# A four-layer kernel with one hand-written order for each engine: the order behind the weight search rewritten, with the chains of batches 2 and 3 between the tiles in small pieces

## What is computed

```python
x = x + _L0_xattn_ref(_layernorm(x), ctx, Wq, bq, Wk, bk)   # attention over the features
x = x + _L0_ffn_ref(_layernorm(x), w_fc, w_proj)            # 256 -> 1024 -> 256, squared relu
x = x + _L1_xattn_ref(_layernorm(x), fside, ctx)            # gated MLP in int8, weights per batch
x = x + _L1_ffn_ref(_layernorm(x), Wq, keys, e_down, e_up)  # product-key lookup of experts

# _L0_ffn: both weights are first quantised: for each block of 64 the best of 16 scales is searched
# _L1_xattn, twice per batch (gate_up, then down):
s = jnp.sqrt(jnp.maximum(amax_x, EPS) / jnp.maximum(amax_w, EPS)); xs = x / s; ws = w * s
x_q = jnp.clip(jnp.round(xs / x_scale), -QMAX, QMAX); w_q = jnp.clip(jnp.round(ws / w_scale), -QMAX, QMAX)
h = x_q @ w_q.T * x_scale * w_scale.T
# _L1_ffn, per token and head (4 heads, 2048 experts):
s1, i1 = top_k(sim1, 8); s2, i2 = top_k(sim2, 8)
final_scores, pk_idx = top_k((s1[:, None] + s2[None, :]).reshape(64), 8)
hidden = silu(x . e_down[idx]) * relu(final_scores); out = sum(hidden * e_up[idx])
```

## Time and profile before

| | us |
|---|---|
| median of 3 runs (lowest, highest) | 453.34 (451.8, 455.67) |
| profiled execution, its own time | 452.77 |
| its span, first to last instruction | 451.0 |
| busy in the span: PE, DVE, ACT, POOL | 372.2, 334.8, 248.1, 164.0 |
| share of TensorE's full clock, mean | 0.924 |

### The profile page before, as it was taken

The page is one execution under the profiler, slowest core; times in us unless marked ns, Lnnn a source line. Parts: engine busy times, 40 slices in busy tenths (PEclk is TensorE's granted clock), DMA queues, the critical chain, the costliest instruction groups (busy, mean ns, idle before and its releaser), DMA issues.

```text
span 451.0 us, 8463 instructions
## 1 busy us (share of the span) xinstructions
PE 372.2 (83%) x3278; PEld 277.3 (61%) x3278; DVE 334.8 (74%) x870; ACT 248.1 (55%) x371; POOL 164.0 (36%) x203
## 2 busy tenths in 40 slices
PE   2987897689979997997469959979899789996467
PEld 1554664345434456996357848858688677885356
DVE  4998599957995975367866976597868799569830
ACT  4889959778868982017545454665565754020000
POOL 3355844478979996000010132060502324011000
PEclk9998999869999999998759969999899998999598
DMA  9910000000000002400000000000000000000000
GB/s 265 362 61 2 0 0 1 0 1 1 0 1 1 0 0 55 134 1 1 0 2 1 1 1 1 1 14 1 13 0 15 1 15 1 13 1 3 12 15 12
DMA packets 11144, 11.42 MB, mean 25 GB/s; under 512 B 608, under 2 KB 10592, under 8 KB 11104
## 3 DMA queue, kind: packets, MB, share of 16 engines
q1 hardware_dynamic: 11104, 10.88, 7.6%
HBM read 9.83 MB, written 1.05 MB: 24 GB/s over the span
## 4 chain that ended last, share of the span: by engine, by line
PE 40%; DVE 25%; ACT 12%; POOL 11%; issue 10%; DMA 1%; POOLq 0%; DVEq 0%; ACTq 0%
PE pair L729 11%; PE pair L693 8%; POOL arena L336 7%; PE pair L555 5%; PE pair L664 4%; PE pair L715 3%; POOL arena L319 3%; DVE arena L1232 2%; PE pair L677 1%; DVE i L1431 1%; PE pair L515 1%; PE pair L393 1%; ACT arena L1063 1%; DVE arena L1227 1%; DVE arena L1506 1%
## 5 line engine op out<-in xcount | busy, mean ns | idle before, releaser
L336 POOL TENSOR_TENSOR arena<-arena 128x512 f32<-128x512 f32 x64 | 91.1, 1434 | 53.0 <-ACT arena L940 21.4
L729 PE MATMUL pair<-EU,arena 128*128 128x256 f32 x256 | 62.0, 400 | 11.4 <-DVE arena L1512 9.3
L693 PE MATMUL pair<-arena,EDT 128*128 128x256 f32 x256 | 60.3, 385 | 4.0 <-ACT arena L1071 4.0
L729 PEld LDWEIGHTS pair<-EU,arena 128*128 128x128 f32 x256 | 50.9, 202 | 18.8 <-DVE arena L1506 11.5
L377 POOL TENSOR_TENSOR arena<-arena 128x512 f32<-128x512 f32 x20 | 26.1, 1327 | 90.6 <-ACT arena L1063 90.6
L1232 DVE TENSOR_REDUCE arena<-arena 128x16 f32<-128x512 f32 x64 | 42.7, 678 | 20.7 <-POOL arena L336 20.6
L515 PE MATMUL pair<-QP,nidentr 128*128 128x512 f32 x144 | 46.9, 450 | 13.1 <-ACT arena L937 10.4
L693 PEld LDWEIGHTS pair<-arena,EDT 128*128 128x128 f32 x256 | 47.2, 190 | 11.6 <-ACT arena L1071 5.4
L515 PEld LDWEIGHTS pair<-QP,nidentr 128*128 128x128 f32 x144 | 27.1, 203 | 25.6 <-issue 18.0
L940 ACT ACTIVATE arena<-pair 128x1024 f32<-128x1024 f32 x32 | 33.4, 1043 | 13.9 <-PE pair L522 13.9
L522 PE MATMUL pair<-arena 128*128 128x512 fp8e4 x128 | 40.3, 398 | 0.0
(11 more groups left out here) (195 smaller groups left out, 649.7 us busy)
## 6 DMA issues: line engine op xcount, KB each, us to landing
arena<-in_L_ffn_e_down_dram SPq DMA_DIRECT2D x1, 2048.0 KB, 12.2
EU<-in_L_ffn_e_up_dram SPq DMA_DIRECT2D x1, 2048.0 KB, 8.1
arena<-in_L_ffn_w_fc_dram SPq DMA_DIRECT2D x2, 512.0 KB, 5.3
X<-in_x_dram SPq DMA_DIRECT2D x1, 1024.0 KB, 6.0
arena<-in_L_ffn_w_proj_dram SPq DMA_DIRECT2D x1, 1024.0 KB, 13.7
GUW<-in_fside_BxS2xS_dram SPq DMA_DIRECT2D x1, 1024.0 KB, 11.5
out_dram<-arena SPq DMA_DIRECT2D x8, 128.0 KB, 2.2
CTX<-in_ctx_dram SPq DMA_DIRECT2D x1, 512.0 KB, 4.9
```

The lines of the kernel that those rows point to most:

```text
L336: pool.tensor_tensor(qf(g), sq[:, :, 0:32], sq[:, :, 32:64], ALU.add).then_inc(s["folded"], 1)
L693: last = pe.matmul(bk2(4 + i % 2)[:, r, :], EDT[:, k, at:at + P], xT4[:, b % 2, k, :], start=(k == 0), stop=(k == 1))
L729: last = pe.matmul(bk2(7)[:, n, :], PR[:, n, e, :], EU[:, e, :], start=(e == 0), stop=(e == EROWS - 1))
```

## The change

Only the order of calls changes, on PE, ACT, DVE and POOL, from the end of the search on; SP's list is as it was. The same helpers are called for the same batches and tiles. The loop is gone; the calls are written out one by one, and some are split further: `experts` and `up` into pieces of 1 to 16, `coefficients_out` and `weigh` by quarters, for which `weigh` gets an argument on both engines. The waits that were inside `ffn2` and `c_x_transposed` now stand in the list of calls; the wait for `x3` of an earlier batch, for `c_pre` and `c_ratio` before a `pre`, and for `d_xT_e` behind it keep the shared bank 6 apart. `mask` waits in addition for its own engine's previous `one_hots`. Cut to its core:

```diff
-            def weigh(t):
+            def weigh(t, quarters):
 
                 b, i = t // 2, t % 2
                 pool.wait_ge(s["d_g_e"], 8 * b + 8)
                 gv = G[:, b % 2, :, i * P:i * P + P].rearrange("p e (s g) -> p e s g", s=4)
                 pv = PR[:, i, :, :].rearrange("p e (s g) -> p e s g", s=4)
-                for q in range(4):
+                for q in quarters:
                     half, r = q // 2, q % 2
                     pool.wait_ge(s["d_c_e"], 4 * t + q + 1)
                     w = pv[:, :, 2 * r:2 * r + 2, 16 * half:16 * half + 16]
                     pool.tensor_tensor(w, w, gv[:, :, 2 * r:2 * r + 2, 16 * half:16 * half + 16], ALU.mult
                                        ).then_inc(s["d_weighed"], 1)
...
-            for t in range(NT):
-                if 0 < t <= DVE_WEIGHS:
-                    weigh(t - 1)
-                ranks(t)
-                coefficient_parts(t)
+            coefficient_parts(0)
+            ranks(0)
+            coefficient_parts(1)
+            ranks(1)
+            weigh(0, (0, 1, 2, 3))
+            ranks(2)
+            coefficient_parts(2)
+            weigh(1, (0,))
+            ranks(3)
+            weigh(1, (1, 2))
+            coefficient_parts(3)
...
 
-            pe.wait_ge(s["wT_e"], 6)
-            pe.wait_ge(s["hsq"], 16)
-            ffn2(2, 0)
-            ffn2(3, 0)
-            gate_weights_transposed(0)
-            ffn2(0, 0)
-            w_transposed(NCH - 1)
-            gate_weights_transposed(1)
-            pe.wait_ge(s["wT_e"], 8)
...
+            pe.wait_ge(s["wT_e"], 6)
+            pe.wait_ge(s["hsq"], 16)
+            gate_weights_transposed(0)
+            ffn2(1, 0)
+            ffn2(0, 0)
+            w_transposed(NCH - 1)
+            pe.wait_ge(s["wT_e"], 8)
             ffn2(0, 1).then_inc(s["f2_t"], 1)
-            ffn2(1, 0)
+            ffn2(1, 1).then_inc(s["f2_t"], 1)
             c_x_transposed(0)
-            ffn2(1, 1).then_inc(s["f2_t"], 1)
+            ffn2(3, 0)
             c_factors(0)
-            ffn2(2, 1).then_inc(s["f2_t"], 1)
+            ffn2(2, 0)
+            gate_weights_transposed(1)
+            gate_weights_transposed(2)
+            ffn2(2, 1, (0,))
+            gate_weights_transposed(3)
...
             half_queries(0, 0, 1)
             c_a_transposed(1)
             half_queries(0, 1, 2)
+            c_factors2(1)
             sims(0, 0)
-            experts(0, 0, 2)
-            c_factors2(1)
-            experts(0, 2, 4)
+            experts(0, 0, 1)
             c_row_scales2(1)
-            experts(0, 4, 5)
+            c_factors(2)
             c_quantised2_transposed(1)
-            experts(0, 5, 6)
+            sims(0, 1)
+            experts(0, 1, 2)
             c_second(1)
+            experts(0, 2, 6)
+            pe.wait_ge(s["c_pre"], 3)
+            pre(1)
             experts(0, 6, 8)
-            for b in range(B - 2):
-
-
-                sims(b, 1)
-                scatter(b, 0, 0)
-                pre(b + 1)
-                c_x_transposed(b + 2)
-                scatter(b, 0, 1)
-                half_queries(b + 1, 0, 2)
-                experts(b + 1, 0, 2)
-                c_factors(b + 2)
-                up(b, 0, 0, EROWS)
-                experts(b + 1, 2, 3)
-                c_row_scales(b + 2)
-                experts(b + 1, 3, 4)
-                c_quantised_transposed(b + 2)
-                sims(b + 1, 0)
-                c_first(b + 2)
-                scatter(b, 1, 0)
-                experts(b + 1, 4, 5)
-                c_a_transposed(b + 2)
-                scatter(b, 1, 1)
...
-                c_row_scales2(b + 2)
-                up(b, 1, EROWS // 4, EROWS // 2)
-                c_quantised2_transposed(b + 2)
-                up(b, 1, EROWS // 2, EROWS // 4 * 3)
-                c_second(b + 2)
-                up(b, 1, EROWS // 4 * 3, EROWS)
-
-            sims(B - 2, 1)
-            scatter(B - 2, 0, 0)
-            pre(B - 1)
...
-            experts(B - 1, 0, 2)
-            up(B - 2, 0, 0, EROWS)
-            scatter(B - 2, 1, 0)
-            sims(B - 1, 1)
-            experts(B - 1, 2, 5)
-            scatter(B - 2, 1, 1)
-            experts(B - 1, 5, 8)
-            up(B - 2, 1, 0, EROWS)
-            for n in range(TPB):
-                scatter(B - 1, n, 0)
-                scatter(B - 1, n, 1)
-                up(B - 1, n, 0, EROWS)
+            pe.wait_ge(s["d_xT_e"], 2)
+            c_row_scales(2)
+            half_queries(1, 0, 2)
+            scatter(0, 0, 0)
+            sims(1, 0)
+            c_quantised_transposed(2)
+            experts(1, 0, 1)
+            scatter(0, 0, 1)
+            c_first(2)
+            experts(1, 1, 2)
+            c_a_transposed(2)
+            experts(1, 2, 3)
+            sims(1, 1)
+            pe.wait_ge(ld["eu"], 16)
+            up(0, 0, 0, 4)
+            c_factors2(2)
+            experts(1, 3, 5)
+            scatter(0, 1, 0)
+            experts(1, 5, 6)
+            c_row_scales2(2)
+            up(0, 0, 4, 8)
+            c_quantised2_transposed(2)
+            scatter(0, 1, 1)
+            c_second(2)
+            up(0, 0, 8, 16)
+            pe.wait_ge(s["x3"], 3)
+            c_x_transposed(3)
+            experts(1, 6, 8)
+            pe.wait_ge(s["c_ratio"], 4)
+            pre(2)
+            up(0, 1, 0, 4)
+            pe.wait_ge(s["d_xT_e"], 3)
+            c_factors(3)
+            up(0, 1, 4, 8)
+            half_queries(2, 0, 2)
+            scatter(1, 0, 0)
+            c_row_scales(3)
+            sims(2, 0)
+            experts(2, 0, 1)
+            c_quantised_transposed(3)
+            scatter(1, 0, 1)
...
+            c_row_scales2(3)
+            experts(2, 4, 5)
+            c_quantised2_transposed(3)
+            experts(2, 5, 6)
+            c_second(3)
+            experts(2, 6, 8)
+            scatter(2, 0, 0)
+            up(1, 1, 0, 4)
+            pre(3)
+            scatter(2, 0, 1)
+            half_queries(3, 0, 2)
+            experts(3, 0, 1)
+            sims(3, 0)
+            up(1, 1, 4, 16)
+            sims(3, 1)
+            experts(3, 1, 2)
+            scatter(2, 1, 0)
+            experts(3, 2, 3)
+            up(2, 0, 0, 8)
+            scatter(2, 1, 1)
+            up(2, 0, 8, 16)
+            experts(3, 3, 8)
+            scatter(3, 0, 0)
+            scatter(3, 0, 1)
+            up(2, 1, 0, 16)
+            scatter(3, 1, 0)
+            scatter(3, 1, 1)
+            up(3, 0, 0, 16)
+            up(3, 1, 0, 16)
...
 
             def mask(t):
 
+                if t:
+                    dve.wait_ge(s["d_onehot"], t)
                 dve.wait_ge(s["d_packed"], t + 1)
                 dve.tensor_tensor(msk, iotaJ.unsqueeze(1).to_broadcast([P, NO, JW, NG]), over(t, 0, JW), ALU.is_equal
                                   ).then_inc(s["d_mask"], 1)
@@ -1489,16 +1571,17 @@
                 dve.tensor_tensor(wc, msk.unsqueeze(1).to_broadcast([P, 3, NO, JW, NG]), parts, ALU.mult
                                   ).then_inc(s["d_onehot"], 1)
 
-            def weigh(t):
+            def weigh(t, quarters):
 
                 b, i = t // 2, t % 2
                 dve.wait_ge(s["d_g_e"], 8 * b + 8)
-                dve.wait_ge(s["d_weighed"], 4 * t)
+                if quarters[0] == 0:
+                    dve.wait_ge(s["d_weighed"], 4 * t)
                 if t >= 2:
                     dve.wait_ge(s["d_up_t"], t - 1)
                 gv = G[:, b % 2, :, i * P:i * P + P].rearrange("p e (s g) -> p g s e", s=4)
...
+            c_clip(2)
             one_hots(0)
-            x3(1)
-            ln_apply(1, 2, "ln4")
-            for b in range(B - 2):
-                t = 2 * b
-                if b:
-                    result(t - 1)
-                top8(t + 1)
-                c_ratio(b + 2)
-                pair_top8(t + 1)
-                c_factor(b + 2)
-                look_up(t + 1)
-                c_round(b + 2)
-                mask(t + 1)
-                c_clip(b + 2)
-                one_hots(t + 1)
-                c_h(b + 2)
-                result(t)
-                c_a(b + 2)
-                top8(t + 2)
-                c_ratio2(b + 2)
-                pair_top8(t + 2)
-                c_factor2(b + 2)
-                look_up(t + 2)
-                c_round2(b + 2)
-                mask(t + 2)
-                c_clip2(b + 2)
-                one_hots(t + 2)
-                x3(b + 2)
-                ln_apply(b + 2, 2, "ln4")
-
-            result(NT - 5)
-            top8(NT - 3)
-            for t in (NT - 3, NT - 2):
-                pair_top8(t)
-                look_up(t)
-                mask(t)
-                one_hots(t)
-                top8(t + 1)
-                if t == NT - 3:
-                    result(t - 1)
-                    weigh(t)
-            pair_top8(NT - 1)
-            look_up(NT - 1)
-            mask(NT - 1)
-            weigh(NT - 2)
-            result(NT - 3)
-            one_hots(NT - 1)
```

(37 more changed lines are left out.)

241 lines of the change are left out of this document (163 added, 78 removed).

## The result

After takes 423.31 us (median of 4 runs, 422.9 to 425.79); before took 452.99 beside it (451.8 to 455.67, 4 runs). The ratio is 0.9336, 95% interval 0.9304 to 0.9368: 6.6% faster, some 29.7 us. The profiled execution took 423.64 us with a span of 421.8 (before 452.77 and 451.0). The page and the stages, cut at 266 us, where I had put the first scatter (it starts at 262.92), and at 402, shortly before `up` of tile 6 (403.79). The last line is the whole work behind the search, from its first row on PE at 171.85.

The account below looks back on a forecast made before the run. No engine alone was taken as the bound, but PE and DVE waiting for each other. First scatter 266, plus 126.4 + 3.0 + 6.0 + 3.5, plus end 17.6, plus 1.8 around the span: 424.3 us, range 413.5 to 441.

Parts of the forecast that it names:

- DVE's +10.0 us: Before the first scatter: DVE has 12.6 us more chain work, less about 2.6 moved ahead, delaying one_hots(0).
- The lead that it buys: Chain of batch 2: c_clip(2) done at about 262 us, was 285.9; the chain is 24 us ahead.
- 126.4 us of work: PE from first scatter to up of tile 6: scatters, sims, experts, up, queries and short chain pieces, at warm prices.
- 3.0 of issue stalls: PE's new end: a 1.49 us stop between back-to-back scatter halves, expected twice.
- 6.0 of waits: PE before up of tile 6: c_a(2) 0.8, coefficient quarter 0.8, up of tile 1 1.3, scatter(1,0,0) 2.7, tile 7 0.4.
- 3.5 of slip: DVE before up of tile 6: lateness from hand-overs and POOL's weighing holding DVE, with bounds for POOL of 0 and 26.6 us.
- at warm prices: PE's work from the first scatter to up of tile 6 priced without a slow clock.
- The slower rival: Tiles: one_hots behind later chain steps makes every scatter late; scatter(1,0,0) from 322 on, time 460.6 us; chance 0.06.
- DVE becomes the bound: Tiles: POOL's quarters hold DVE half their length each, 13 us in place of 3.5, time 434 us; chance 0.14.
- 17.6 us from `up` of tile 6 on: The end: two up calls of 7.0 each, result and hand-over 0.8, last result 0.2 + 0.4, store 2.2.
- Only the end gains: Rival: the middle stays at 51.6 us a batch, 15.7 us go at the end, time 437.1 us; chance 0.08.
- the rest from the batch period: Split of the 28.5 us gain: some 11 from waits at the end, 4 from clock there, the rest here.

Follow-up runs that it names:

- e11: After with mask(0), one_hots(0), experts(0,6..8) and scatter(0,0,0) moved ahead of chain steps, so the first tile starts earlier: 425.36 us, ratio 0.9367 to before.
- e2: Before with chain 1 served first where it meets the first tile, c_factors2(1) ahead of sims(0,0) and two experts on PE: 452.99 us, ratio 0.9981.
- e1: Before with one call moved on PE, ffn2(2,0) behind c_factors(0), so that x2(0) comes earlier: 452.29 us, ratio 0.9974.
- e6: After with POOL's weighing cut to one of 16 expert rows per quarter, same instructions and waits: 418.49 us, ratio 0.9242 to before.
- e8: After with all of POOL's weigh(4) behind ranks(6), off the one-hots of tile 5: 423.99 us, ratio 0.9373 to before.
- e5: After with PE's last seven calls back in the order of before, DVE's list unchanged: 437.40 us, ratio 0.962 to before.
- e3: Before with weigh(6) and result(5) ahead of the top-8 work of tile 7 on DVE: 447.58 us, ratio 0.9859.
- e10: Before with the new order of the end on PE and DVE and the old loop, result(6) left ahead of weigh(7): 455.52 us, ratio 1.0036.
- e7: After with one_hots(2) ahead of c_round(3) on DVE, and chain 3's steps on PE and ACT behind the tile's calls: 424.31 us, ratio 0.9374 to before.
- e12: After with POOL's weigh(2, (2, 3)) and weigh(3, (0,)) behind coefficient_parts(4), and weigh(4) whole behind ranks(6): 428.72 us, ratio 0.9432 to before.
- e9: Before with c_clip(b+2) and c_clip2(b+2) moved behind the one-hots on DVE in its loop: 454.45 us, ratio 1.0015.
- e4: Before with three edits together: ffn2(2,0) later, chain 1 served first, weigh(6) ahead of tile 7's top-8 work: 446.52 us, ratio 0.987.

## Why the prediction was right

I said 424.3 us with a range of 413.5 to 441; it is 423.31. The total is nearer than its terms deserve.

**The front.** I had c_factors2(1) at 236.8 and scatter(0,0,0) at 266; they stand at 233.15 and 262.92, c_clip(2) at 258.5 and not 262. Of the 3.1 us at the scatter 2.2 are the earlier end of the search, which I had put at 174.03 "as before". Of the 1.5 us that are left of c_factors2(1)'s 3.6, 0.9 is the clock: the first half of the queries took 2.87 us where before took 3.78. DVE's +10.0 us between sims(0,0) and the scatter was +10.4: 262.92 - 234.20 = 28.7 us after, 258.16 - 239.80 = 18.4 before. The lead that it buys was right too: c_clip(2) comes 258.5 - 171.85 = 86.7 us into the stretch and came 285.51 - 174.03 = 111.5 us into it, 24.8 us earlier, and I had said 24. By themselves these pieces are worth little: an earlier first scatter (e11) and the exchange in PE's queue (e2) gave nothing, and the earlier x2(0) (e1) one or two microseconds.

**PE's work from there on.** I summed 126.4 us of work, 3.0 of issue stalls, 6.0 of waits and 3.5 of slip: 138.9 us from the first scatter to `up` of tile 6. It took 403.79 - 262.92 = 140.9. Waits and stalls came to 1.11 + 0.76 + 1.61 + 2.27 + 1.80 + 1.47 = 9.0, not 12.5; the work was 5.4 longer, so two errors met and left 2 us. 3.6 of that are two stretches at a slow clock which I had ruled out with "at warm prices":

```profile
310.00:314.00 4.00, 4.00 (x80) 0.68 0.02 4
394.00:398.00 4.00, 4.00 (x14) 0.65 0.00 0
```

In the first, sims(2,0) and the experts behind it took 1.96 and 2.81 us in place of 1.1 and 1.9; in the second, `up` of tile 5 took 8.86 for 7.07. Of the waits, those for c_a(2) (1.11), for a coefficient quarter (0.76) and at scatter(1,0,0) (2.27) were foretold; that before `up` of tile 1 stood one call earlier, before pre(2), as 1.61 us for c_ratio(3) in place of 1.3 for result(0); the 1.80 at scatter(1,1,0) I had not found. The issue stall came once (1.47), not twice: the scatters of tile 7 ran 192 products in 2.57 us without a stop.

**scatter(1,0,0)** started at 309.35, to be compared with 311; add the 2.2 us of the search and it is 311.5. The slower rival, which wanted 322, was dead at that row, and the first scatters stand 46.4 us apart and not 56.3. e11 adds that an earlier first scatter does not bring the end nearer.

**POOL and DVE.** This term was somewhat too small. I took 3.5 us with hand-overs included. With most of POOL's weighing removed (e6) 4.3 us of the time go, or 5.6 of the stretch with the clock set aside (7.3 - 1.7), and PE's shorter waits there add up to 4.45 us. I had argued that many of the quarters still fall under top8; four of the twenty lay beside the one-hots. The waits of 1.61 and 1.80 us, counted above among the 9.0, are part of this price. The rival "DVE becomes the bound" was right that POOL holds DVE up; its price of 13 us was more than twice what it came to, and DVE is not the bound throughout, since 2.2 us of it given back at tile 5 gained nothing (e8).

**The end.** 17.6 us from `up` of tile 6 on; measured 421.8 - 403.79 = 18.0. The two calls took 7.6 (with the small stop) and 7.14 us, near the 7.0 that I had priced. From 311 us to the end PE is busy 94% of the time, where I had said over 90:

```profile
311.00:421.80 110.80, 104.02 (x1508) 0.97 0.03 10
```

"Only the end gains" (437.1) fell with the middle: without the new order of PE's end 15.4 us of the stretch are gained (e5).

**What the sum of causes looks like.** I split the 28.5 us into 11 of waits at the end, 4 of clock there and the rest from the batch period. By position that is near: up to `up` of tile 6 the stretch is 17.5 us shorter, behind it 9.5 (from my numbers 18.6 and 9.9), and e5 puts 13.3 of the 27.0 us ahead of scatter of tile 6. "From the batch period" is only a part of the cause, though: 5 us of the middle are the queries of batches 1 to 3 at the full clock, which I had priced but not named in the split. And the two parts lean on each other. On the old middle, weighing tile 6 earlier gives 6.4 us (e3), and the new end on PE and DVE gave nothing as run (e10); on the new middle, PE's new end gives 12.9 us by e5, or some 9 with e5's mismatch set aside. The whole change gives 30.1 by the ratio. The cover at the end is `up` of tile 5, and it can be held back only when the lists are already so far ahead that scatter of tile 6 need not wait for its one-hots: in e10 that scatter waited 6.43 us, in after it did not wait. I had added the two as if they were independent; by how much they are not, e5 and e10 leave open, each for the flaw named.

The main thing stays open: whether the middle's gain comes from the lead of the chains, from the finer pieces, or from both was not taken apart. The lead is seen in the trace (24.8 us, no wait of DVE for ACT's rounding), and e7, where chain 3 gave its lead away and the waits came back, speaks for it; no run shows what it is worth. And no order that I tried (e7, e8, e11, e12) beat after: the intervals of their ratios overlap with its own, or lie above it (e12).

## What to carry to other kernels

When two engines are each some 80% full and wait for each other, a wait in the trace is not a price: three waits that I could name (5.2, 3.66 and 2.48 us) gave nothing when the work at that one place was exchanged, since what was moved had been the cover of the next step (e9) or stood in the next step's way (e2). What paid here is a whole whose pieces were not priced apart: lead, by a thin chain started a batch earlier with its steps between pieces of other work that nobody wants soon, and a last block of full-engine work kept for the place where only one list runs.

Before moving a wait, ask what the moved work was hiding; before delaying work on a side engine, ask who waits for it (e12: 1.80 us taken away, 3.87 us put in its place). And compare executions from the first instruction at which the orders differ: here 2.2 us of the profiled gain lay ahead of it.

## What the runs showed of the hardware

**The clock of an unchanged part differs.** The same instructions of the search ran on PE at a granted clock of 0.50 in the stretch from 90 to 98 us of before:

```profile
90.00:98.00 8.00, 6.24 (x10) 0.50 0.00 1
```

In after that stretch was at 1.00, in e3, e5, e6 and e10 at 0.51 to 0.53, in e4 and e7 at 0.58 and 0.59, and in e1, e2, e8, e9, e11 and e12 at 0.79. The product at L493 (L515 in after) there took 3.68 us before and 1.98 in after, and the search ends 0.9 to 2.2 us earlier in the executions with the higher clock (172.56 to 173.16 for those at 0.79). e5 and e6 share after's order and have the low clock (0.52), so it isn't the order of the calls; what decides it I don't know, and one profiled execution of each can't say whether it goes with the kernel or with the run.

**A busy engine can be at the slow clock for a while.** `up` of tile 5 in after ran 4 us at 0.65 while PE was fully busy, behind a single stop of 1.47 us. The same call took 8.86 us in e7 behind a stop of 1.20 and 8.80 in e8 behind 1.37, but 7.17 us in e6, e11 and e12 behind stops of 1.35, 1.28 and 1.20: the length of the stop does not tell which comes. In e10 `up` of tile 5 took 9.72 us, 4 us after a wait of 6.43 had ended. The price of idle time is paid later than the idle time, by other instructions, and not always.

**The issue stall inside a double scatter** (1.0 to 1.6 us, with nothing released) doesn't go with the place alone either. Before and e3 have it in both doubles of the end, after, e6 and e10 in the first only, e5 in the second only. I had counted it at each.
